# Local attention on one core: where the mask is added, who applies layer norm's scale and bias, and where the third gate matmul stands

## The reference, cut to what matters

```python
sim = einsum(bq, bk2) * 8.0
sim = where(mask, -finfo.max, sim)
attn = softmax(sim, -1)
out = einsum(attn, bv2)
...
xn = (x - mu) / sqrt(var + 1e-05) * g + bln
a, gate = split(xn @ W1 + b1, 2, -1)
x = a * gelu(gate) @ W2 + b2 + x
```

## Time and profile before

| | us |
|---|---|
| median of three runs (2365.16 to 2367.01) | 2366.53 |
| the profiled execution | 2368.98 |
| span of its trace | 2367.2 |

### The profile page before, as it was taken

One profiled execution on the slowest core, in us unless ns is written; L12 is line 12 of the kernel. 1 busy time (PEld: TensorE's weight loads), 2 busy tenths in 40 slices (PEclk: granted clock), 3 DMA queues, 4 the chain that ended last, 5 costly groups with the idle time before them and its releaser, 6 DMA issues. The chain is left out here.

```text
span 2367.2 us, 65878 instructions
## 1 busy us (share of the span) xinstructions
PE 2123.9 (90%) x26476; PEld 1010.9 (43%) x26476; DVE 1585.3 (67%) x2054; ACT 1753.6 (74%) x2574; POOL 1096.7 (46%) x461
## 2 busy tenths in 40 slices
PE   8699999999999999999999999999998687678697
PEld 3244444444444444444444444444443222223365
DVE  5566676666676676666666766767665589998432
ACT  4688878888888888888888788888886565455443
POOL 0255555455555555555555555555552025565030
PEclk8899999999999999999999999999999889999799
DMA  0332233322323223332233222333221100000011
GB/s 23 109 108 86 93 107 99 102 90 95 115 89 105 90 95 113 101 95 91 87 118 104 92 91 86 115 103 100 87 90 47 41 0 0 0 0 1 19 35 37
DMA packets 102070, 181.03 MB, mean 76 GB/s; under 512 B 15904, under 2 KB 67504, under 8 KB 101680
## 3 DMA queue, kind: packets, MB, share of 16 engines
q1 hardware_dynamic: 101776, 176.83, 23.2%
HBM read 24.73 MB, written 1.05 MB: 11 GB/s over the span
## 5 line engine op out<-in xcount | busy, mean ns | idle before, releaser
L767 POOL TENSOR_TENSOR f_shuf<-f_shuf,f_tabs 128x1024 f32<-128x1024 f32 x192 | 467.7, 2436 | 866.0 <-DMA f_shuf<-f_raw 866.0
L772 POOL TENSOR_TENSOR f_rot<-f_rot,f_shuf 128x1024 f32<-128x1024 f32 x192 | 452.8, 2358 | 15.1
L814 DVE TENSOR_REDUCE f_max<-f_ps 128x8 f32<-128x512 f32 x192 | 132.7, 691 | 302.4 <-PE f_ps L514 294.5
L670 ACT ACTIVATE f_rn<-f_ps 128x1024 f32<-128x1024 f32 x192 | 195.9, 1021 | 134.0 <-PE f_ps L492 134.0
L798 DVE TENSOR_TENSOR f_rot<-f_ps,f_tabc 128x1024 f32<-128x1024 f32 x192 | 235.1, 1225 | 51.9 <-ACT f_raw L660 49.3
L492 PE MATMUL f_ps<-f_sq,f_same 64*64 64x256 f32 x3072 | 210.1, 388 | 44.1 <-DVE f_rot L798 43.5
L806 DVE SCALAR_TENSOR_TENSOR f_qk<-f_rn,f_rot 128x1024 f32<-128x1024 f32 x192 | 233.4, 1216 | 9.5 <-POOL f_rot L772 8.0
L672 ACT ACTIVATE f_rn<-f_rn,k_lift 128x1024 f32<-128x1024 f32 x192 | 220.6, 1149 | 6.3
L480 PE MATMUL f_ps<-y_t,f_wq 128*128 128x512 f32 x384 | 217.1, 647 | 8.3 <-issue 5.5
L1200 POOL TENSOR_TENSOR s_prod<-s_state,s_cs 128x1024 f32<-128x1024 f32 x64 | 151.7, 2370 | 146.9 <-DVE s_state L1278 146.9
L824 DVE TENSOR_REDUCE f_sum<-f_ps 128x8 f32<-128x512 f32 x192 | 132.7, 691 | 119.8 <-ACT f_ps L688 119.5
(11 more groups left out here) (262 smaller groups left out, 3551.9 us busy)
## 6 DMA issues: line engine op xcount, KB each, us to landing
f_shuf<-f_raw SPq DMA_DIRECT2D x384, 256.0 KB, 2.4
f_rn<-f_rn SPq DMA_DIRECT2D x384, 128.0 KB, 2.4
e_w<-in_e_w SPq DMA_DIRECT2D x16, 256.0 KB, 2.9
f_wq<-in_f_wq SPq DMA_DIRECT2D x12, 256.0 KB, 3.4
f_wk<-in_f_wk SPq DMA_DIRECT2D x12, 256.0 KB, 4.1
f_wv<-in_f_wv SPq DMA_DIRECT2D x12, 256.0 KB, 4.0
f_wo<-in_f_wo SPq DMA_DIRECT2D x6, 512.0 KB, 4.8
f_w<-in_f_w SPq DMA_DIRECT2D x6, 341.0 KB, 4.1
```

The source lines that it names most:

```text
L767: pool.tensor_tensor(view(w, 0, [S, 4], [1, S]), view(w, 0, [S, 4], [1, S]), view(tab_s, 0, [S, 2], [0, 2], [1, S]), ALU.mult).then_inc(se ...
L772: pool.tensor_tensor(t[:, :], t[:, :], w[:, :], ALU.add).then_inc(sem["rot"], 1)
```

## The change

The mask matmuls and the bf16 copies of mask and identity go; the scores start their own accumulation. VectorE adds the mask in PSUM ahead of the row maximum. Layer norm's scale is folded into the VectorE product in slot 4, its bias is added by a second VectorE instruction behind it, and the ScalarE instruction goes. The third gate matmul moves from the end of slot 5 to the place ahead of that slot's norms, and the gelus run in the order 2, 0, 1; the waits on gelus are renumbered: values(0) now wait for the second, mix(4) for the third, `hid_mm` 0 for the first.

```diff
+        GBANK, GFIRST = (2, 7, 3), 2
...
                 if q == 0:
-                    need(pe, sem["gelu"], i * 3 - 6 + 1 + G0)
+                    need(pe, sem["gelu"], i * 3 - 6 + 2 + G0)
...
-                for h in range(2):
-                    pe.matmul(view(ps, (4 + h) * CH, [1, 256]), identb[:, :], maskb[:, :], start=True, stop=False,
-                              skip_group_check=True)
...
-                                       t[64 * h:64 * h + 64, WIN * w:WIN * w + WIN], keys, start=False, stop=True,
+                                       t[64 * h:64 * h + 64, WIN * w:WIN * w + WIN], keys, start=True, stop=True,
...
                 if j == 4:
-                    gather(sem["gelu"], i * 3 - 3 + 2 + G0)
+                    gather(sem["gelu"], i * 3 - 3 + 3 + G0)
...
             def hid_mm(i, f):
                 if f == 0:
-                    need(pe, sem["gelu"], i * 3 + 3 + G0)
+                    need(pe, sem["gelu"], i * 3 + 1 + G0)
...
+                if before and j == 5:
+                    gate_mm(k, GFIRST)
...
                     gate_mm(k, 0)
                     gate_mm(k, 1)
-                    gate_mm(k, 2)
...
-                if before and j == 5:
-                    need(act, sem["scaled"], k + 1)
-                    act.activation(xn[:, :], xn[:, :], ACT.Identity, scale=fcol[:, 0:1], bias=fcol[:, 1:2]).then_inc(sem["xn"], 1)
...
-                    for f in range(3):
+                    for f in (GFIRST, 0, 1):
                         gelu(k, f)
...
                 need(dve, sem["s_mm"], i * 8 + j + 1)
+                dve.tensor_tensor(view(ps, 4 * CH, [CH, 2], [1, S]), view(ps, 4 * CH, [CH, 2], [1, S]),
+                                  view(mask, 0, [0, 2], [1, S]), ALU.add).then_inc(sem["masked"], 1)
+                need(dve, sem["masked"], i * 8 + j + 1)
...
-                    dve.tensor_tensor(xn[:, :], cen[:, :], bank(3), ALU.mult).then_inc(sem["scaled"], 1)
+                    dve.scalar_tensor_tensor(out=xn[:, :], in0=cen[:, :], scalar=fcol[:, 0:1], in1=bank(3),
+                                             op0=ALU.mult, op1=ALU.mult).then_inc(sem["scaled"], 1)
+                    need(dve, sem["scaled"], k + 1)
+                    dve.tensor_scalar(xn[:, :], xn[:, :], fcol[:, 1:2], None, ALU.add).then_inc(sem["xn"], 1)
...
-            dve.tensor_copy(maskb[:, :], mask[:, :])
-            dve.tensor_copy(identb[:, :], ident[:, :]).then_inc(sem["zero"], 1)
```

More of the change, by code:

```diff
@@ L318, in local_attention @@
         mask, halves = m.sb("f_mask", 4 * 64), m.sb("f_halves", 2)
-        maskb = m.mem.enter_context(nc.sbuf_tensor("f_maskb", [128, 4 * 64], mybir.dt.bfloat16))
-        identb = m.mem.enter_context(nc.sbuf_tensor("f_identb", [128, C], mybir.dt.bfloat16))
         v = m.sb("f_v", 8 * CH)
@@ L338, in local_attention @@
             "shift exp sum rcp p t_mm ptz pv_mm o wo_mm y1 mean cen sq2 var ln2 rs2 scaled xn g_mm gelu h_mm hid "
-            "w2_mm y2 fcol tab seen cross0 cross1").split()}
+            "w2_mm y2 fcol tab seen masked cross0 cross1").split()}
         bank = lambda k, n=1: view(ps, k * CH, *([[CH, n]] if n > 1 else []), [1, CH])
@@ L347, in local_attention @@
         Y0, H0_, G0 = NU, 1, 1
-        GBANK = (2, 7, 3)
+        GBANK, GFIRST = (2, 7, 3), 2
         n2_out = o[:, T:2 * T]
@@ L500, in scores @@
                 gather(sem["p"], i * 8 + j)
-                if isinstance(i, int) and i + j == 0:
-                    pe.wait_ge(sem["zero"], 2)
-                    pe.sem_inc(sem["seen"], 1)
                 t = qk[j % 2]
-                for h in range(2):
-                    pe.matmul(view(ps, (4 + h) * CH, [1, 256]), identb[:, :], maskb[:, :], start=True, stop=False,
-                              skip_group_check=True)
                 for w in range(UNIT // WIN):
@@ L565, in gate_mm @@
             def gate_mm(i, f):
-                if f == 0:
+                if f == GFIRST:
                     need(pe, sem["xn"], i + 1)
@@ L699, in gelu @@
                 n = FB[f][1]
-                need(act, sem["g_mm"], i * 3 + f + 1)
+                need(act, sem["g_mm"], i * 3 + (f + 1) % 3 + 1)
                 act.activation(gate[0:n, f * UNIT:f * UNIT + UNIT], view(ps, GBANK[f] * CH, [1, CH], rows=n),
@@ L839, in hidden @@
                 need(dve, sem["h_mm"], i * 3 + f + 1)
-                need(dve, sem["gelu"], i * 3 + f + 1 + G0)
+                need(dve, sem["gelu"], i * 3 + (f + 1) % 3 + 1 + G0)
                 dve.scalar_tensor_tensor(out=hid[0:n, f * UNIT:f * UNIT + UNIT], in0=view(ps, 3 * CH, [1, CH], rows=n),
```

## The result

The changed kernel takes 2405.23 us, the median of four runs (2402.60 to 2411.22), beside 2366.77 for the kernel before in the same comparison: a ratio of 1.016, with a 95% interval of 1.0144 to 1.0177. It is slower, by 38.5 us. The profiled execution takes 2407.47, its span is 2405.7.

What follows compares the result with a forecast made beforehand. The chain through the other engines was taken to bound slots 3 and 4, TensorE slots 0 to 2 and 7; +1.10 a turn over 22 turns (+24.2), plus fcols and units, gave +36.2 and 2403 us, range 2371 to 2420.

Steps and rivals of the forecast that it cites:

- scores of slot 0 to scores of slot 3: Output projection slots 0 to 2 stay set by TensorE and save 0.31 us each, -0.93 a turn.
- slot 3: Set by the chain through the other engines, this slot goes from 7.39 to 7.75 us, +0.36.
- scores of slot 4 to its exponential: With the mask add on VectorE this stretch goes from 2.89 to 3.07 us, +0.18.
- to the exponential of slot 5: From slot 4's exponential: the bias, held until GpSimd's L767 ends, makes 7.80 us into 9.46, +1.66.
- to the scores of slot 7: From slot 5's exponential: 0.1 us from ScalarE's removed bias and 0.31 from the mask, -0.41.
- to the next turn: From slot 7's scores: +0.73 to its exponential, then -0.49 to the next turn.
- The mask on TensorE: Removing the mask matmuls saves TensorE 0.31 us a slot, perhaps 0.2 if only the mask hid the scores' weight loads.
- The mask add: VectorE's added instruction ahead of the row maximum takes 0.72 us, so a slot set by the chain takes 7.75.
- The bias: In slot 4, held by GpSimd every time, ending 7.37 us after the exponential; rival without a hold: 2374 us, chance 0.12.
- The gap ahead of the norms: TensorE idles some 2.1 us there in slot 5; rival that the clock falls: 2428 us, chance 0.08.
- Caught fcols: In seven turns where GpSimd holds the fcol instruction, slots 2 to 4 lose 1.17 us more each, +8.2.
- First and last unit: First unit, chain alone, seven slots of +0.36, +2.5; last unit to its norms, +1.3.

Runs made afterwards that it cites:

- layer norm alone: The kernel before with layer norm's scale and bias on VectorE, mask by TensorE, gate at the end of slot 5: 2398.04 us, ratio 1.0138.
- gate put back: The changed kernel with the third gate matmul back at the end of slot 5 and gelus in the old order: 2427.35 us, ratio 1.0256.
- the gate alone: The kernel before with only the third gate matmul moved ahead of norms and the gelus reordered: 2445.87 us, ratio 1.0335.
- the fastest version: Kernel before with layer norm on VectorE, bias from PSUM, gate moved, fcol early, VectorE's mask in slots 0, 1, 2 only: 2349.06 us.
- the mask alone: The kernel before with the mask added by VectorE and nothing else: 2385.08 us, ratio 1.0068.

## Why the prediction was right, term by term

The forecast of 2403 was met by 2405.23, and the mechanism was the one argued for: the chain sets slots 3 and 4, the bias is held, and slot 5 pays. Against the profiled execution the sum gave +36.2 us; the two of them differ by 2407.47 - 2368.98 = 38.5. A plain turn by its steps, all from the starts shown above:

| step | forecast | measured |
|---|---|---|
| scores of slot 0 to scores of slot 3 | -0.93 | 257.30 - 231.56 = 25.74 where 26.39 was: -0.65 |
| slot 3 | +0.36 | 7.79: +0.40 |
| scores of slot 4 to its exponential | +0.18 | 268.16 - 265.09 = 3.07: +0.18 |
| to the exponential of slot 5 | +1.66 | 9.28: +1.48 |
| to the scores of slot 7 | -0.41 | 294.09 - 277.44 = 16.65 where 17.07 was: -0.42 |
| to the next turn | +0.24 | 10.21 where 9.91 was: +0.30 |
| turn | +1.10 | +1.29 |

- **The mask on TensorE** was mis-sized. I took 0.31 a slot; a removed pair gives 0.21. It is near the lower bound of 0.2 that the text named.
- **The mask add** takes 0.698 us (192 rows), where 0.69 to 0.72 was taken, and the slot of 7.75 came out to the hundredth in slot 4. In slot 3 the add waits 0.04 for the residual of slot 2, which stands ahead of it on VectorE.
- **The bias** is held, and the term is 0.18 too large because GpSimd's L757 began 4.54 after the exponential (272.70 - 268.16) instead of 4.72. That it is caught in *every* turn was wrong: in five of 23 rows the transfer that releases GpSimd came late enough for the bias to start first. Slot 5 takes 9.81 in those turns, 1.06 under the median. The Trainium skill, "SBUF — State Buffer", section on the two separate sides, has a VectorE instruction in a two-port mode and a GpSimd instruction share a pair of ports, which the first to start holds for its whole instruction; the rows agree in both directions, with a bias of 1.55 us behind GpSimd and a GpSimd instruction of 2.62 instead of 2.36 us behind the bias.
- **The gap ahead of the norms** was put at 2.1 us and is 1.57, the bias being 0.18 sooner, and another 0.37 being a wait of the projections in slot 5 for ScalarE's logarithm. The clock fell at this place in one turn only (gap of 1.99, slot 5 of 12.85). The experiments show how near it was: with gaps of 1.84 to 2.27 us (layer norm alone) it fell in seven of 23 turns, with gaps of 2.58 and more (gate put back) in eleven of 17.
- **Caught fcols** were put at +8.2 for seven; there are eight, and what slots 3 and 4 take above their medians grew by 8.3 us in 22 turns (9.9 to 18.2).
- **Slot 0 behind a loop branch** is a term that the sum lacks. It takes 11.03, 10.04, 9.93 and 10.38 in the four turns that begin a pass of the loop (before: 9.18 to 9.19). The wait "issue" of VectorE's first instruction there was 7.3 us in four places before, and is 8.8 (longest 2.83) after. Before, a TensorE-bound slot had room for most of it; now the mask add has to pass ahead of the maximum, and over 22 turns slot 0 loses 5.4 us more above its median. That the cost before was covered by slack, I infer from the two traces; no run took the branch away.
- **First and last unit** were put at +2.5 and +1.3; the first gave +1.5 (62.50 for 60.98), the last +1.6 up to its last scores (62.14 for 60.58). The first unit before is no plain one: its first slot ran partly at the lower level (granted clock 0.57 over 99 to 103 us) and takes 8.73, where the next ones take 7.34. In the runs of layer norm alone and of the gate alone, where that slot keeps the full level, the unit takes 59.59 and 59.57. The changed kernel has such a stretch in its second slot (8.08, the next ones 7.75). Without the two the difference would be about 2.6, an estimate: 62.50 - 0.33 - 59.58. What lies ahead of the first scores is 2.1 us shorter, and what lies behind the last ones 2.1 longer; neither is explained here.

These terms sum to the result: 22 plain turns by the medians of their slots 28.2, fcols 8.3, branches 5.4, the five free biases and the other odd turns in slots 5 to 7 -6.4, units 3.1, in all 38.6, where the spans differ by 38.5. So the forecast's nearness owes something to errors of both signs: the mask term too good by 22 x 0.28 = 6 us and the branches left out, against the bias 0.18 x 22 = 4 us too dear and held in five turns too many.

## What to carry to other kernels

Work that goes from a busy engine to an idle one pays only in the stages where the first is what ends last. Here the same mask add costs in the slots that the softmax chain sets and gains 0.21 us in those that TensorE sets, and splitting it by slot gave the fastest version. Before an elementwise instruction is put on VectorE beside a running GpSimd, see where its operands lie: with its source in PSUM the same addition took 0.75 us always, from SBUF to SBUF 0.49 where it was free and 1.54 to 1.98 where it was held. A matmul that is moved into a wait must have its own input ready there.

## What the runs showed of the hardware that I had not expected

- The granted clock fell to 0.72 over 6 us after single idle stretches of 1.87 and 2.58 us in slot 5, in a program that is otherwise nearly always at the full level in the units. It is no matter of the gap alone. In the 22 turns of each run, no gap up to 1.63 us ahead of the norms was followed by the lower level; of the 24 between 1.84 and 2.27 us, 8 were; of the 39 between 2.52 and 3.51 us, ahead of the norms or of the moved gate, 27 were. So were two behind a loop branch, of 1.55 and 1.73 us. What decides at equal gaps was not settled.
- VectorE's hold by GpSimd works the other way round too: L757 took 2.61 to 2.63 instead of 2.36 us in the five turns in which the bias came first, and 2.35 to 2.37 where that bias read PSUM.
- The parts of the change do not add up: the mask alone cost 0.68%, layer norm alone 1.38%, the gate alone 3.35%, and the three together 1.6%. Alone, the gate waits for its input, and behind that wait and behind the one of layer norm alone the clock falls.
